# Mixing the values of a 16-head attention kernel in array tiles of 128 rows by 32 columns instead of 64 by 32

## What is computed

```python
scores = jnp.einsum('nqhd,nkhd->nhqk', Q, K) * scale     # q, k: heads; h: token
attn = jax.nn.softmax(scores, axis=-1)
out = jnp.einsum('nhql,nlhd->nqhd', attn, V)             # the mixing of values
return jnp.einsum('nse,fe->nsf', out.reshape(n, s, e), Wo) + bo
```

## Time and profile before

| | |
|---|---|
| Time, median of 3 runs | 1617.57 us (1615.98 to 1618.86) |
| The profiled execution: its own time | 1617.31 us |
| Its span, first to last instruction | 1615.6 us |
| Busy: PE, DVE, ACT, POOL | 1574.3, 1352.2, 962.2, 1388.3 us |
| Instructions on PE (matmuls) | 22566 |

### The profile page before, as it was taken

How to read it: one execution, slowest core, us unless ns; L and a number is a source line. 1 busy time by engine, 2 the same in 40 slices (tenths; PEclk the granted TensorE clock), 3 DMA queues, 4 the chain that set the end, 5 groups by cost and what they waited for, 6 DMA issues and landing times.

```text
span 1615.6 us, 59515 instructions
## 1 busy us (share of the span) xinstructions
PE 1574.3 (97%) x22566; PEld 918.5 (57%) x22566; DVE 1352.2 (84%) x2476; ACT 962.2 (60%) x2009; POOL 1388.3 (86%) x1429
## 2 busy tenths in 40 slices
PE   8899999999999999999999999999999999999993
PEld 3455555555555555555555555555555555555551
DVE  7678888888888888888888888888888888888888
ACT  5445665665665665665665665665665665665654
POOL 4668988988988988988988988988988988988967
PEclk9999999999999999999999999999999999999996
DMA  6656766767767766766767766766766767766652
GB/s 228 181 138 188 199 160 201 199 160 201 200 159 200 199 160 200 200 158 202 197 161 202 200 157 202 199 159 202 198 160 202 198 159 203 196 159 203 161 147 75
DMA packets 388653, 293.72 MB, mean 182 GB/s; under 512 B 296854, under 2 KB 296854, under 8 KB 388380
## 3 DMA queue, kind: packets, MB, share of 16 engines
q1 hardware_dynamic: 345936, 223.54, 52.1%
q10 hardware_dynamic: 42444, 66.37, 13.1%
HBM read 155.46 MB, written 67.24 MB: 138 GB/s over the span
## 4 chain that ended last, share of the span: by engine, by line
PE 92%; POOL 3%; DVE 2%; ACT 1%; issue 1%; DMA 0%; ACTq 0%; POOLq 0%; SPq 0%; DVEq 0%
PE ps_q L1330 7%; PE ps_v L1330 7%; PE ps_y L1429 7%; PE ps_q L1336 7%; PE ps_v L1336 7%; PE ps_y L1431 7%; PE ps_q L1345 7%; PE ps_v L1345 7%; PE ps_y L1434 6%; PE ps_s L1384 6%; PE ps_o L1406 5%; PE ps_k L1320 4%; PE ps_k L1330 4%; PE ps_k L1322 4%; PE ps_k L1336 3%; PE ps_k L1324 3%
## 5 line engine op out<-in xcount | busy, mean ns | idle before, releaser
L1115 ACT ACTIVATE q_sb<-ps_q,qk_back 128x512 f32<-128x512 f32 x127 | 87.6, 689 | 356.3 <-PE ps_q L1345 354.4
L486 POOL TENSOR_TENSOR o_sb<-o_sb,x 128x512 f32<-128x512 f32 x122 | 153.7, 1278 | 95.7 <-ACT o_sb L1066 95.5
L451 POOL TENSOR_TENSOR x_t<-x_t,mr_row 128x512 f32<-128x512 f32 x126 | 195.5, 1552 | 6.6 <-DMA mr_row<-x_d 4.5
L458 POOL TENSOR_TENSOR x_t<-x_t,mr_row 128x512 f32<-128x512 f32 x126 | 196.5, 1559 | 0.5
L739 DVE SCALAR_TENSOR_TENSOR x<-ps_y,y_back,bo_row 128x512 f32<-128x512 f32 x125 | 93.8, 750 | 99.4 <-PE ps_y L1434 99.4
L464 POOL TENSOR_TENSOR xT_lo<-x_t,xT_hi 128x512 f16<-128x512 f32 x127 | 164.0, 1292 | 6.8 <-ACT xT L1083 6.7
L474 POOL TENSOR_TENSOR x<-x,res 128x512 f32<-128x512 f32 x124 | 161.1, 1299 | 3.3 <-ACT x L1066 3.3
L1330 PE MATMUL ps_v<-wv_hi,xT_hi 128*128 128x512 f32 x508 | 162.4, 441 | 1.4 <-ACT v_tok L1122 1.4
L728 DVE STREAM_TRANSPOSE qT<-q_sb 128x512 f32<-128x512 f32 x128 | 134.5, 1051 | 34.0 <-ACT q_sb L1115 34.0
L1330 PE MATMUL ps_q<-wq_hi,xT_hi 128*128 128x512 f32 x508 | 161.4, 439 | 0.6 <-issue 0.6
L1429 PE MATMUL ps_y<-wo_hi,oT_hi 128*128 128x512 f32 x500 | 160.9, 443 | 0.0
(11 more groups left out here) (221 smaller groups left out, 3653.6 us busy)
## 6 DMA issues: line engine op xcount, KB each, us to landing
x_in<-in_xa SPq DMA_DIRECT2D x64, 512.0 KB, 6.4
x_t<-in_xt SPq DMA_DIRECT2D x64, 512.0 KB, 8.6
k_bd<-kT SPq DMA_DIRECT2D x512, 64.0 KB, 3.0
v_d<-v_tok ACTq DMA_DIRECT2D x128, 256.0 KB, 2.6
v_key<-v_d SPq DMA_DIRECT2D x128, 256.0 KB, 4.4
res<-in_xr SPq DMA_DIRECT2D x64, 512.0 KB, 5.5
p_bd<-pT ACTq DMA_DIRECT2D x500, 64.0 KB, 2.7
out<-o_sb SPq DMA_DIRECT2D x62, 512.0 KB, 7.4
```

What stands on the lines that cost most here:

```text
L451: nc.gpsimd.tensor_tensor(x_t[v % 2][:, j, :, :], x_t[v % 2][:, j, :, :], mr_row[v % 2][:, :, 0, j].unsqueeze(1).to_broadcast([P, EC, P]), ...
L458: nc.gpsimd.tensor_tensor(x_t[v % 2][:, j, :, :], x_t[v % 2][:, j, :, :], mr_row[v % 2][:, :, 1, j].unsqueeze(1).to_broadcast([P, EC, P]), ...
L486: nc.gpsimd.tensor_tensor(o_sb[:, v % 2, j, :], o_sb[:, v % 2, j, :], x1[:, v % 3, j, :], ALU.add).then_inc(out_done, 1)
```

## The change

The mixing takes 128 rows by 32 columns of the array a matmul: all 128 partitions of `v_key` are held in one of four column strips, and 128 columns of `p_bd` are streamed, four diagonal blocks of 32. A tile has 16 such matmuls instead of 32. `p_bd` has four blocks a tile instead of two (its zeroing covers twice the size; the copies into it move the same data to other places). A tile's result fills one bank, `ps_o[:, t % 2, :]`, and who reads it waits for that tile alone. In the main loop `spare` stands at seven places instead of four, with 26 or 27 instead of 14.

```diff
-        p_bd = sb("p_bd", [P, 2, 2, E])
+        p_bd = sb("p_bd", [P, 2, 4, E])
...
-            return ps_s[:, :, half_of(0)] if t == NT - 1 else ps_o[:, :, half_of(t)]
+            return ps_s[:, 0, :] if t == NT - 1 else ps_o[:, t % 2, :]
...
-        def mixed_by(t):
-            return NT - 1 if t == NT - 2 else both(t)
...
-                    nc.scalar.dma_start(p_bd[rows, t % 2, c % 2, :], pT[t % 2][rows, :, :].rearrange("p n h -> p (n h)")
+                    nc.scalar.dma_start(p_bd[rows, t % 2, c, :], pT[t % 2][rows, :, :].rearrange("p n h -> p (n h)")
...
-                dve.wait_ge(ohi_done, 2 * mixed_by(t))
+                dve.wait_ge(ohi_done, 2 * (t + 1))
...
-                act.wait_ge(o_ready, mixed_by(t))
-                nc.scalar.activation(o_turned(t)[0][:, :, :].rearrange("p a (r n) -> p r a n", r=2),
-                                     mixed_in(t).rearrange("p r (a n) -> p r a n", a=EC), ACT.Copy
+                act.wait_ge(o_ready, t + 1)
+                nc.scalar.activation(o_turned(t)[0][:, :, :],
+                                     mixed_in(t).rearrange("p (a n) -> p a n", a=EC), ACT.Copy
...
-                        for r in range(2):
-                            half = slice(64 * r, 64 * r + 64)
-                            mm = nc.tensor.matmul(to[32 * g:32 * g + 32, r, a * 64:a * 64 + 64],
-                                                  v_key[t % 2][half, 4 * g + a, :], p_bd[half, t % 2, :, 32 * n:32 * n + 32],
-                                                  start=True, stop=True, tile_position=(64 * r, 32 * g), skip_group_check=True)
+                        mm = nc.tensor.matmul(to[32 * g:32 * g + 32, a * P:(a + 1) * P], v_key[t % 2][:, 4 * g + a, :],
+                                              p_bd[:, t % 2, :, 32 * n:32 * n + 32], start=True, stop=True,
+                                              tile_position=(0, 32 * g), skip_group_check=True)
...
                 keys(a)
+                spare(26)
                 queries(a)
-                spare(14)
+                spare(26)
                 values(a)
-                spare(14)
+                spare(26)
                 keys(b)
-                spare(14)
+                spare(26)
                 output(a - 4)
-                spare(14)
+                spare(26)
                 queries(b)
+                spare(27)
                 values(b)
+                spare(27)
                 output(b - 4)
```

More of the change, by code:

```diff
@@ L314, in probs_half_out @@
                     rows = slice(32 * c, 32 * c + 32)
-                    sp.dma_start(p_bd[rows, t % 2, c % 2, :], pT[t % 2][rows, :, :].rearrange("p n h -> p (n h)")
+                    sp.dma_start(p_bd[rows, t % 2, c, :], pT[t % 2][rows, :, :].rearrange("p n h -> p (n h)")
                                  ).then_inc(p_moved[t % 2], DMA)
@@ L778, in o_low @@
             def o_low(t):
-                dve.wait_ge(ohi_done, 2 * mixed_by(t))
-                nc.vector.tensor_tensor(o_turned(t)[1][:, :, :].rearrange("p a (r n) -> p r a n", r=2),
-                                        mixed_in(t).rearrange("p r (a n) -> p r a n", a=EC),
-                                        o_turned(t)[0][:, :, :].rearrange("p a (r n) -> p r a n", r=2).bitcast(F32),
+                dve.wait_ge(ohi_done, 2 * (t + 1))
+                nc.vector.tensor_tensor(o_turned(t)[1][:, :, :],
+                                        mixed_in(t).rearrange("p (a n) -> p a n", a=EC),
+                                        o_turned(t)[0][:, :, :].bitcast(F32),
                                         ALU.subtract).then_inc(olo_done, 1)
@@ L1129, in o_high @@
             def o_high(t):
-                act.wait_ge(o_ready, mixed_by(t))
-                nc.scalar.activation(o_turned(t)[0][:, :, :].rearrange("p a (r n) -> p r a n", r=2),
-                                     mixed_in(t).rearrange("p r (a n) -> p r a n", a=EC), ACT.Copy
+                act.wait_ge(o_ready, t + 1)
+                nc.scalar.activation(o_turned(t)[0][:, :, :],
+                                     mixed_in(t).rearrange("p (a n) -> p a n", a=EC), ACT.Copy
                                      ).then_inc(ohi_done, 1)
-                nc.scalar.activation(o_turned(t)[2][:, :, :].rearrange("p a (r n) -> p r a n", r=2),
-                                     mixed_in(t).rearrange("p r (a n) -> p r a n", a=EC), ACT.Copy
+                nc.scalar.activation(o_turned(t)[2][:, :, :],
+                                     mixed_in(t).rearrange("p (a n) -> p a n", a=EC), ACT.Copy
                                      ).then_inc(ohi_done, 1)
```

## The result

The changed kernel takes 1651.43 us (median of 4 runs, 1651.07 to 1651.58) against 1617.07 for the kernel before on the same chip (4 runs): a ratio of 1.0211, 95% interval 1.0199 to 1.0224. The prediction was 1652.7, in 1638 to 1670.

The account below looks back on a forecast made before the run. PE, busy 97% of the span, was taken to bound the kernel. On 1617.3 us came +35.9 for 63 pairs' mixing and tiling change, -1 for fetching and +0.5 for the tail: 1652.7 us, range 1638 to 1670.

Parts of the forecast that it names:

- Streaming: In a pair's mixing, each place streams 16 instructions of 0.111 us, 1.78 us where it was 1.34: +0.44 us a pair.
- the half-clock mixing: Last tiles' mixing at 1.2 GHz: starts 13.6 ns apart, eight places streaming without pause, so columns are the limit there.
- the exposed weight load: Rival in the mixing: the 27 ns a place is unhidden weight load, 0.93 us a pair, +59, so 1676; chance 10%.
- the number of instructions: Rival in the mixing: each instruction costs 10.1 ns whatever it streams, -32 us over 63 pairs, so 1586; chance 6%.
- the pause of a place: In the old mixing at 2.4 GHz, 81 ns between a place's instructions, 54 of them streaming, leaving 27 ns.
- The change of tiling: Between scores and mixing, which no longer share a tiling: 0.04 us of lost overlap and 0.09 of waiting, +0.13 a pair.
- Sum over a pair: Streaming and change of tiling in the mixing together: 0.57 us a pair, +35.9 us over 63 pairs.
- Empty instructions at nothing: In the loop, going from 56 to 184 empty instructions a round costs nothing, hidden behind streaming projections.
- Fetching: Instruction fetching in the loop: the late queries go away, between 0 and -2 us, taken as -1.
- The tail: Last two tiles' mixing, 0.19 us longer at full clock and 0.74 at 1.2 GHz; half taken, +0.5 us.
- At nothing: Off PE's path: 1.8 us more zeroing of `p_bd` on POOL and ACT's 45.7 us wait for the mixing change no time.

Follow-up runs that it names:

- The half-column run: The changed kernel with its mixing streaming only 64 of the 128 columns, half of each mixed tile left out: 1599.25 us, ratio 0.989 to the kernel before.
- the run in turn: A round's first stages reordered to scores, mixing, scores, mixing: 1668.52 us in the changed kernel, 1617.14 us in the kernel before.
- the old empty instructions: The changed kernel with the kernel before's empty instructions, 14 at four places of a round: 1650.7 us, ratio 1.0209 to the kernel before.

## Why the prediction was right

*Streaming*, 16 x 0.111 = 1.78 us and 1.9 with the end: 1.88 to 1.89 measured. The step that carried it was reading the half-clock mixing as proof that columns, not weights or instructions, set the pace once they are long enough. The half-column run confirms it by itself. The rival of the exposed weight load (2.24 with the end) and that of the number of instructions (0.75) fall with the same row. One working is loose: half of 0.111 is 0.056 and not the 0.054 that the prediction took for 64 columns, so the pause of a place at full clock was 25 ns and not 27; at half the clock 109 ns then stand against 111, and the reading stays.

*The change of tiling*, +0.13: measured 0.13, and 0.14 a change in the run in turn. The two changes that the round had already were the right rows for it.

*Sum over a pair*, +0.57: measured +0.60 a round. Of the 0.03 that the sum lacks, over half is in the mixing (1.887 against 1.430 us as the median of the rounds, +0.457 and not +0.44). The rest stands behind it: the keys' float32r group lasts 1.13 us (838.54 to 839.67 on the timeline), before 1.12. It is there with the old empty instructions too, so they are not its cause; what is stays open.

*Empty instructions at nothing*: right for 26, but the margin was not seen. The tail's 0.67 us showed only that 26 vanish. At 0.071 us each and 0.25 on top, some 34 (an estimate from those two numbers) fill the 2.67 us of a projection, and 45 at seven places cost over 5 us a round.

*Fetching*, -1: the late queries are gone, as forecast. After the second, no round is over 24.83 us, where six had 0.2 more, so 1.2 us came back; in the first the queries start 0.68 us behind the keys' last group (70.01 to 70.69), where they were 0.96 late, while the stop in the mixing stays. So some -2 us in all. The mechanism, named only as a queue, is blocks of 256 entries of PE's list.

```profile
64.33 0.63 PE L1401 MATMUL ps_o<-p_bd,v_key 128*32 128x128 f32 x13
66.55 1.72 PE L1401 MATMUL ps_o<-p_bd,v_key 128*32 128x128 f32 x51 [1.58 <-issue]
...
70.01 1.04 PE L1321 MATMUL ps_k<-wk,xT_lo 128*128 128x512 f16 x4
70.69 1.28 PE L1327 MATMUL ps_q<-wq_hi,xT_hi 128*128 128x512 f32 x4
```

*The tail*, +0.5: the one term with the wrong sign, and further off than it looks, because two of the 63 pairs are mixed behind the loop too. The forecast for that stretch was 2 x 0.57 + 0.5 = +1.6. From the loop's end to the last instruction the kernel before needs 71.0 us (1544.65 to 1615.6) and the changed one 70.6, so -0.4. Two things were wrong. The 0.74 us for the last tile rested on half a clock, and that did not come: PE now waits 1.74 us before it instead of 2.88, and the granted clock there is 1.00. So PE reaches its last group of matmuls 43.3 us after the loop's end (1622.51) and not 46.1 (1590.73) as before. And PE's time is not what the tail costs: it came 2.8 us earlier and the end only 0.4, and the chain that ended last runs there mostly over POOL, in both kernels.

```profile
1614.08 1.08 PE L1401 MATMUL ps_o<-p_bd,v_key 128*32 128x128 f32 x32
1616.90 1.08 PE L1401 MATMUL ps_s<-p_bd,v_key 128*32 128x128 f32 x32 [1.74 <-issue]
...
1622.51 1.03 PE L1429 MATMUL ps_v<-wo,oT_lo 128*128 128x512 f16 x4
```

and in the kernel before:

```profile
1590.73 1.03 PE L1434 MATMUL ps_v<-wo,oT_lo 128*128 128x512 f16 x4
```

The window around the last tile's mixing with the change:

```profile
1616.80:1618.00 1.20, 1.10 (x33) 0.93 (x33) 1.20 (x3) 1.13 (x4) 0.92 (x3) 1.00 0.30 51
```

*At nothing*: the zeroing of `p_bd` took 3.51 us instead of 1.80, and the idle time behind it shrank from 5.67 to 4.34. ACT's wait for the mixing fell from 45.7 to 29.3 us in all, and DVE's wait for ACT's reads of it (`o_low`) from 31.8 to 3.8. PE is 93% of the chain, so neither sets the pace.

```profile
6.68 3.51 POOL L541 MEMSET p_bd<- 128x4096 f32 x1
14.54 2.22 POOL L466 TENSOR_SCALAR wk<-x,w_scale 128x1024 f16<-128x1024 f32 x2 [4.34 <-DVE w_back L696]
...
  ACT oT_hi L1128: 29.3, 59
```

*The total*: the profiled execution took 1651.5 us against 1652.7, closer than its terms came, and that is luck. The loop was forecast at 61 x 0.57 - 1 = +33.8 and grew by 34.7, 0.9 more; the stretch behind it came out 2.0 below its forecast. The two misses cancel in part. The mechanism and its two large terms, streaming and the change of tiling, were right by themselves.

## What to carry to other kernels

Fewer, larger matmuls are no gain where they use fewer places of the array at once: multiply the columns by the instructions of one place, and compare that with what the count of instructions costs (here 10 ns each). Keep neighbouring stages in the same tiling, or pay 0.14 us a change. And where an unrolled list of PE has a dense stretch, a change in its length elsewhere can cost far more than the change itself: take an edit that adds or removes instructions together with its effect on where the 256-entry blocks begin.

## What the runs showed of the hardware that was not expected

- The length of PE's list in a round decides over up to 10% of the time. The kernel before runs at 1617 us with 768 entries a round, 1775 with 712 and 1805 with 896; the changed one at 1651 with 768 and 640, 1691 with 584. Stops of up to 2.9 us between two starts stand at multiples of 256 entries that fall into or shortly behind scores and mixing. With 896 entries part of the loss is not theirs but that of the half clock behind them and of the empty instructions. Such a place is harmless at 768 entries (the first round stops behind 13 matmuls of the mixing, the later ones do not), and there the transfer comes early: in one round of the kernel before, the last transfer ahead of the boundary in the mixing (818.45 us) ran from 815.46 to 816.39, 2.1 us before it, and nothing stops. In a round with 712 entries it ran from 817.65 to 819.10, the mixing was at the boundary by 818.2 and went on at 820.60. What lets the transfer start earlier at 768 is open.
- An empty instruction takes PE's sequencer 0.071 us, far more than the 10 ns of a matmul with its weight load. Behind a projection 26 cost nothing.
- With one strip after the other the mixing took 4.26 us a pair. Were matmuls to start in the order in which the program lists them, eight of one strip in a row would need 7 x 0.107 us before the next strip starts, 4 x 7 x 0.107 = 3.0 us a tile and 6.0 a pair. The trace has 4.26, and in it the next strip begins before the last three of a strip's eight instructions have started. So PE starts some out of that order. The Trainium skill (TensorE: Matmul & The Clock Gate, The mechanism) has matmuls start and end in strict program order; this run does not agree with it, unless the order was changed when the kernel was compiled, which the trace does not tell.
